# Order of the turnings and of GpSimd's subtraction in a two-stream attention kernel

## The reference

```
xn  = layernorm(x)
# linear attention ("s"), 16 heads of 32
q,k = softmax(ln(xn)@Wq+bq), softmax(ln(xn)@Wk+bk)        # each head by itself
v,p = split(ln(xn)@W_in)
k   = (1-smear)*k + smear*k_of_the_token_before
o   = tril(q k^T * decay) v / (row sum + eps)
s   = ln(silu(p)*o @ W_out)
# local stream ("g"), two layers, 8 heads of 64, windows of 128 tokens and the one before
h   = shift_token(x); q,k,v = split(h@wqkv)
q,k = rotary(l2norm(q)), rotary(l2norm(k))
x   = x + softmax(mask(8 q k^T)) v @ wo
h   = ln(shift_token(x)); x = x + (a*gelu(g))@w2,  a,g = split(h@w1+b1)
out = x_in + s * silu(g stream)
```

## Time and profile before

| | |
|---|---|
| median of 3 runs | 1975.97 us (1974.36 to 1982.03) |
| the profiled execution's own time | 1983.42 us |
| its span | 1981.6 us |
| TensorE matmul busy | 1906.0 us, 96% |
| TensorE weight loads busy | 1645.8 us, 83% |
| VectorE busy | 1732.8 us, 87% |
| ScalarE busy | 1224.2 us, 62% |
| GpSimd busy | 1018.6 us, 51% |
| granted TensorE clock | 0.995 |

### The profile page before, as it was taken

The page is one execution under the profiler, slowest core; times in us unless marked ns, Lnnn a source line. Parts: engine busy times, 40 slices in busy tenths (PEclk is TensorE's granted clock), DMA queues, the critical chain, the costliest instruction groups (busy, mean ns, idle before and its releaser), DMA issues.

```text
span 1981.6 us, 49031 instructions
## 1 busy us (share of the span) xinstructions
PE 1906.0 (96%) x15178; PEld 1645.8 (83%) x15178; DVE 1732.8 (87%) x5212; ACT 1224.2 (62%) x2926; POOL 1018.6 (51%) x1004
## 2 busy tenths in 40 slices
PE   5899999999999999999999999999999999999998
PEld 3788888888888888888788888888888888888887
DVE  5888899898889898889888898889899898898896
ACT  4565656656656656656666567566566566566564
POOL 2545555556556555555444455454554554454552
PEclk8999999999999999999999999999999999999999
DMA  5010000000000100000111111110111111111101
GB/s 199 20 33 21 29 25 22 30 29 22 25 29 21 32 29 21 26 26 25 65 62 47 40 34 41 34 32 29 42 32 40 37 32 29 40 34 34 37 26 33
DMA packets 81152, 72.76 MB, mean 37 GB/s; under 512 B 13484, under 2 KB 74344, under 8 KB 81096
## 3 DMA queue, kind: packets, MB, share of 16 engines
q1 hardware_dynamic: 81096, 72.05, 11.8%
HBM read 42.64 MB, written 16.78 MB: 30 GB/s over the span
## 4 chain that ended last, share of the span: by engine, by line
PE 61%; issue 12%; DVE 12%; ACT 6%; POOL 6%; DVEq 1%; DMA 1%; SPq 0%; POOLq 0%; ACTq 0%
PE bank L1521 36%; PE bank L1526 14%; PE bank L1533 10%; ACT L944 2%; POOL rot_other L707 2%; PE bank L1568 2%; POOL mix_work L715 2%; DVE rot L1413 1%; DVE prob L1048 1%; ACT gel L944 1%; DVE mix_work L1431 1%; POOL small_h L663 1%; DVE sq_sum L1305 1%; POOL small_y L663 1%; DVE mix_work L1112 1%
## 5 line engine op out<-in xcount | busy, mean ns | idle before, releaser
L1521 PE MATMUL bank<-hT_n,w_s 128*128 128x128 f32 x3072 | 402.2, 281 | 1.6 <-ACT hT_n L907 0.9
L1521 PEld LDWEIGHTS bank<-hT_n,w_s 128*128 128x128 f32 x3072 | 364.7, 191 | 35.2 <-issue 21.4
L824 ACT ACTIVATE prob<-prob,row_min 128x256 f32<-128x256 f32 x512 | 256.7, 504 | 171.2 <-DVE row_min L1048 169.6
L1526 PE MATMUL bank<-wqkv_s,xT 128*128 128x512 f32 x1152 | 319.2, 413 | 4.6 <-DVE wqkv_s L1225 1.8
L663 POOL TENSOR_TENSOR inv_norm<-sq_clip,half_neg 128x8 f32<-128x8 f32 x128 | 270.3, 2112 | 55.5 <-DVE sq_clip L1308 55.4
L707 POOL TENSOR_TENSOR rot_other<-raw,rot_t 128x256 f32<-128x256 f32 x256 | 190.2, 774 | 150.0 <-ACT raw L793 150.0
L1526 PEld LDWEIGHTS bank<-wqkv_s,xT 128*128 128x128 f32 x1152 | 207.4, 191 | 53.6 <-DVE wqkv_s L1225 3.8
L1048 DVE CUSTOM_DVE_ANT_0 prob<-bank,table,inv_norm 128x256 f32<-128x256 f32 x512 | 226.5, 479 | 3.9 <-issue 3.6
L1521 PE MATMUL bank<-w_s,hid 128*128 128x256 f32 x768 | 202.3, 387 | 0.0
L793 ACT ACTIVATE pT<-bank 128x512 f32<-128x512 f32 x256 | 139.7, 606 | 30.3 <-PE bank L1533 30.2
L1533 PE MATMUL bank<-table,prob 128*128 128x128 f32 x1024 | 144.9, 274 | 2.3 <-DVE prob L1067 2.3
(11 more groups left out here) (180 smaller groups left out, 4313.6 us busy)
## 6 DMA issues: line engine op xcount, KB each, us to landing
k_prev<-k_carry SPq DMA_DIRECT2D x32, 224.0 KB, 2.5
x_s<-in_L_attn_x SPq DMA_DIRECT2D x32, 128.0 KB, 2.1
rot_s<-in_rotary SPq DMA_DIRECT2D x64, 64.0 KB, 2.0
rows_normalised<-xh SPq DMA_DIRECT2D x32, 128.0 KB, 1.7
y_n<-rows_normalised SPq DMA_DIRECT2D x32, 128.0 KB, 2.1
x_between_layers<-x SPq DMA_DIRECT2D x32, 128.0 KB, 1.7
s_between_passes<-s_out SPq DMA_DIRECT2D x32, 128.0 KB, 1.7
x_s<-x_between_layers SPq DMA_DIRECT2D x32, 128.0 KB, 2.1
```

Source lines behind the costliest of these rows:

```text
L824: ins = act.activation(prob[:, h, :], prob[:, h, :], ACT.Exp, bias=row_min[:, c:c + 1], scale=-1.0, accum_out=row_sum[:, c:c + 1])
L1521: return pe.matmul(out, lhsT, rhs, start=first, stop=last)
L1526: ins = pe.matmul(out, halved(left[:, a]), halved(right[:, b]), start=first and n == 0, stop=last and n == 2)
```

## The change

In `body` of TensorE the groups of turnings come in the order linear queries, local queries, linear keys; the two tiles of the MLP's second product, which stood behind the linear queries, stand behind the output projection. ScalarE copies them out in the same order. VectorE evicts the linear values right behind the square sums, and clips the square sums in the odd iteration only after the key weights. GpSimd subtracts the maxima ahead of its four rotary products. Nothing is computed that was not before, and no operation is added.

```diff
--- before.py
+++ after.py
@@ -328,14 +328,14 @@
         score_bank = [mix_bank[0], mix_bank[1], att_bank[0], att_bank[2]]
 
 
-        mix_pe = Steps(sem("mix_pe"), "q k v kt qt s0 s1 s2 s3 p o0 o1 gt wout")
+        mix_pe = Steps(sem("mix_pe"), "q k v qt kt s0 s1 s2 s3 p o0 o1 gt wout")
         state_pe = Steps(sem("state_pe"), "st0 st1")
         state_dve = Steps(sem("state_dve"), "st0 st1")
         state_pool = Steps(sem("state_pool"), "sdec")
         rows_pe = Steps(sem("rows_pe"), "xt")
         rows_dve = Steps(sem("rows_dve"), "xl")
-        mix_act = Steps(sem("mix_act"), "xt exp kt qt tanh gt")
-        mix_dve = Steps(sem("mix_dve"), "q k max sum kinv kw v kadd "
+        mix_act = Steps(sem("mix_act"), "xt exp qt kt tanh gt")
+        mix_dve = Steps(sem("mix_dve"), "q k max v sum kinv kw kadd "
                         "s2 qsum qeps s3 s0 s1 p den0 rec0 o0 den1 rec1 o1 go "
                         "ystat yaggr yvar")
         y_dve = Steps(sem("y_dve"), "yn")
@@ -695,6 +695,12 @@
                     pool.tensor_tensor(rot_t[:, :, :, :],
                                        rot_s[:, p, :, :].unsqueeze(2).to_broadcast([P, 4, 2, HD // 2]),
                                        rot_scale[layer(u)][:, :, :, :], ALU.mult).then_inc(proj_pool.done("table"), 1)
+                if one is not None:
+                    n = one
+                    pool.wait_ge(mix_dve.sem, mix_dve.at("max", n))
+                    qk_h = qk.rearrange("p (h d) -> p h d", d=MD)
+                    pool.tensor_tensor(qk_h, qk_h, qk_max[:, :].unsqueeze(2).to_broadcast([P, 2 * MH, MD]),
+                                       ALU.subtract).then_inc(mix_pool.done("sub"), 1)
                 if proj is not None:
                     u = proj
 
@@ -708,12 +714,6 @@
                                                      rot_t[:, 2 + a, s, :].unsqueeze(1).to_broadcast([P, H, HD // 2]),
                                                      ALU.mult)
                     ins.then_inc(proj_pool.done("other"), 1)
-                if one is not None:
-                    n = one
-                    pool.wait_ge(mix_dve.sem, mix_dve.at("max", n))
-                    qk_h = qk.rearrange("p (h d) -> p h d", d=MD)
-                    pool.tensor_tensor(qk_h, qk_h, qk_max[:, :].unsqueeze(2).to_broadcast([P, 2 * MH, MD]),
-                                       ALU.subtract).then_inc(mix_pool.done("sub"), 1)
                 if one is not None:
                     n = one
                     pool.wait_ge(mix_dve.sem, mix_dve.at("kw", n))
@@ -964,17 +964,17 @@
                 if m is not None:
                     last_gates(m)
                 if one is not None:
-                    act.wait_ge(mix_pe.sem, mix_pe.at("kt", one))
-                    copy(kT_mix[:, :, :], mix_bank[0][:, :].rearrange("p (g i) -> p g i", g=MG))\
-                        .then_inc(mix_act.done("kt"), 1)
+                    act.wait_ge(mix_pe.sem, mix_pe.at("qt", one))
+                    copy(qT_mix[:, :, :], mix_bank[1][:, :].rearrange("p (g i) -> p g i", g=MG))\
+                        .then_inc(mix_act.done("qt"), 1)
                 if proj is not None:
                     act.wait_ge(proj_pe.sem, proj_pe.at("qt", proj))
                     copy(halved(qT[:, 0, :, :]), proj_bank[:, :].rearrange("p (g i) -> p g i", g=HP))\
                         .then_inc(proj_act.done("qt"), 1)
                 if one is not None:
-                    act.wait_ge(mix_pe.sem, mix_pe.at("qt", one))
-                    copy(qT_mix[:, :, :], mix_bank[1][:, :].rearrange("p (g i) -> p g i", g=MG))\
-                        .then_inc(mix_act.done("qt"), 1)
+                    act.wait_ge(mix_pe.sem, mix_pe.at("kt", one))
+                    copy(kT_mix[:, :, :], mix_bank[0][:, :].rearrange("p (g i) -> p g i", g=MG))\
+                        .then_inc(mix_act.done("kt"), 1)
                 if proj is not None:
                     act.wait_ge(proj_pe.sem, proj_pe.at("kt", proj))
                     copy(halved(kT[:, 0, :, proj.parity, :]), proj_bank[:, :].rearrange("p (g i) -> p g i", g=HP))\
@@ -1304,6 +1304,8 @@
                 dve.wait_ge(proj_act.sem, proj_act.at("square", u))
                 dve.tensor_reduce(sq_sum[:, :], rot[:, :].rearrange("p (h d) -> p h d", d=HD), AX_X, ALU.add)\
                    .then_inc(proj_dve.done("sqsum"), 1)
+            def square_clip(u):
+
                 dve.wait_ge(proj_dve.sem, proj_dve.at("sqsum", u))
                 dve.tensor_scalar(sq_clip[:, :], sq_sum[:, :], 1e-24, None, ALU.max)\
                    .then_inc(proj_dve.done("clip"), 1)
@@ -1377,6 +1379,9 @@
                     scores("b1", a, att_bank[0])
                 if one is not None:
                     square_sums(u)
+                    dve.wait_ge(mix_pe.sem, mix_pe.at("v", one))
+                    dve.tensor_tensor(v_mix[:, :, 0:MD], heads(mix_bank[0][:, :]), heads(bias_mix[:, 0, :]),
+                                      ALU.add).then_inc(mix_dve.done("v"), 1)
                 if f is not None:
                     finish_u(f)
                     if one is None:
@@ -1387,6 +1392,7 @@
                     mix_read(two, 0)
                 if u is not None and one is None:
                     square_sums(u)
+                    square_clip(u)
                 if a is not None:
                     weigh("b1", a)
                 if one is not None:
@@ -1400,11 +1406,9 @@
                     dve.tensor_tensor(k_smear[:, :], k_norm[:, :], smear_s[:, :], ALU.mult)
                     dve.tensor_tensor(k_keep[:, :], k_norm[:, :], keep_s[:, :], ALU.mult)\
                        .then_inc(mix_dve.done("kw"), 1)
+                    square_clip(u)
                     if f is not None:
                         finish_out(f)
-                    dve.wait_ge(mix_pe.sem, mix_pe.at("v", one))
-                    dve.tensor_tensor(v_mix[:, :, 0:MD], heads(mix_bank[0][:, :]), heads(bias_mix[:, 0, :]),
-                                      ALU.add).then_inc(mix_dve.done("v"), 1)
                 if a is not None:
                     low_out(a, 0, "pva", "la")
                 if u is not None:
@@ -1810,21 +1814,21 @@
                 if m is not None and one is None and i.low != UNITS:
                     mlp_out(m, 0, 2)
                 if one is not None:
+                    pe.wait_ge(mix_act.sem, mix_act.at("exp", one))
+                    pe.wait_ge(mix_dve.sem, mix_dve.at("k", one))
+                    transposes(mix_bank[1], [qk[:, g * P:(g + 1) * P] for g in range(MG)])\
+                        .then_inc(mix_pe.done("qt"), 1)
+                if u is not None:
+                    turn_q(u)
+                if one is not None:
                     pe.wait_ge(mix_dve.sem, mix_dve.at("kadd", one))
                     pe.wait_ge(mix_dve.sem, mix_dve.at("v", one))
                     transposes(mix_bank[0], [qk[:, ME + g * P:ME + (g + 1) * P] for g in range(MG)])\
                         .then_inc(mix_pe.done("kt"), 1)
-                if u is not None:
-                    turn_q(u)
-                if one is not None:
-                    pe.wait_ge(mix_act.sem, mix_act.at("exp", one))
-                    pe.wait_ge(mix_dve.sem, mix_dve.at("k", one))
-                    transposes(mix_bank[1], [qk[:, g * P:(g + 1) * P] for g in range(MG)])\
-                        .then_inc(mix_pe.done("qt"), 1)
-                    if m is not None:
-                        mlp_out(m, 0, 2)
                 if a is not None:
                     out_projection(a, att_bank[1])
+                if m is not None and one is not None:
+                    mlp_out(m, 0, 2)
                 if i.low == UNITS:
 
                     hidden(m, mlp_bank[0], 2, 4, 2).then_inc(mlp_pe.done("ga"), 1)
```

## The result

| | before | after |
|---|---|---|
| median of 4 runs each | 1977.12 us (1974.36 to 1982.03) | 1953.74 us (1948.87 to 1955.20) |
| ratio, 95% interval | | 0.9875 (0.9848 to 0.9901) |
| the profiled execution, span | 1983.42, 1981.6 us | 1948.87, 1947.0 us |
| VectorE busy, GpSimd busy | 1732.8, 1018.6 us | 1734.0, 1060.6 us |

The change is faster by 23.4 us (1.2%) by the medians, 20 to 30 us by the interval. The forecast was 30 us (1946). Whole runs differ by more than the terms in question, so the experiments are read by another measure: the length of a steady pair of iterations, from one start of the linear query projection (`wq_s`) on TensorE to the next. In the kernel before it is 59.85 us in the first layer (the twelve pairs lie between 59.82 and 59.90) and 60.11 in the second (60.07 to 60.14). After, it is 59.43 and 58.98.

A forecast was written before the change was run, and what follows sets the result against it. TensorE was taken to bound the kernel, itself bound in the odd iteration by VectorE's way to `kadd`. Gains of 10.4, 15.0 and 5 us, taken as 30, came off the median 1975.97: 1946 us, range 1936 to 1967.

The forecast's parts named there:

- The order, 0.91 a pair: TensorE, odd iteration: two groups of turnings move into the gap before the linear keys, gaining 0.91 us even if `kadd` stays.
- even with VectorE unchanged this wait is met, by 0.0 to 0.1 us: TensorE's local key turnings, asked at 1215.22, find the queries' low part ready, as it ends at 1215.09.
- `kadd` earlier by 0.1 to 0.2: VectorE's addition of the shifted linear keys, for which TensorE waits, ends 0.1 to 0.2 us earlier.
- The term of the weighings: VectorE's two weighings of the last heads, beside the last two rotary products, take 1.4 to 1.6 us.
- The second bound: The DMA of the shifted keys, second landing near 1211.65, lets `kadd` end no earlier than about 1212.3.
- The second layer, 14 by 1.07: Fourteen second-layer pairs of iterations gain 1.07 us each, 15.0 us in all.
- The first layer, 13 by 0.8: Thirteen first-layer pairs gain 0.8 us each, 10.4 us in all; the gap of 0.70 to 0.89 goes whole.
- `xh`, whose race with the subtraction I had bounded: VectorE's first-layer step behind the maxima: 0.4 us or less; if it loses, held 1.9 us and gain 0.5, not 0.8.
- The MLP's move, at nothing: TensorE: the MLP's second matmul group goes behind the output projection, the same work, with VectorE's residual input earlier.
- Edges, 5: Five edge pairs of iterations gain 1.0 us each, 5 us in all.
- The second and fourth: Rivals: the gap only moves, nothing won, 1976 us, chance 0.09; more than forecast, up to 40.4 us, 1936, chance 0.08.
- Of the first: Rival: part of the gain is lost to VectorE, last weighing 0.3 to 0.5 us late; gain 14 us, 1962, chance 0.15.

The follow-up runs named there:

- e5: The changed kernel with GpSimd's decayed keys made to wait for VectorE's scaling of the local keys: pairs 58.90 and 58.72 us, ratio 0.9796.
- e6: The changed kernel with the local queries' two rotary products ahead of GpSimd's subtraction: pairs 58.60 and 59.16 us, one run of 1937.82 us.
- e10: The changed kernel with the MLP's two tiles back ahead of the output projection: pairs 59.53 and 59.64 us, one run of 1966.64 us.

## Why the prediction was right, and where not

The direction and the main mechanism were right, the range (1936 to 1967) held the time, and the size was too large by 7 us by the medians (30 against 23), or by 1 to 6 at an equal clock.

- *The order, 0.91 a pair.* It gave 0.61 and 0.65. In the second layer the step that failed is "even with VectorE unchanged this wait is met, by 0.0 to 0.1 us": the weight loads of the local key turnings wait 0.4 us, and 0.26 of the gain is gone. In the first layer the gap (0.70 to 0.89) set the limit, as forecast, and a wait for L1112 in the even iteration took 0.28 of matmul idle back. For the second layer the lines were there to read: the norm in front of the low part missed `k_dec` by 0.08 us, and the decayed queries behind it waited for the very copy that the change makes earlier. I had priced VectorE's steps up to `kadd` and left those behind it as they were. The prediction named this wait as "what is late next", and a new wait of the local keys above 0.3 us as a sign of being wrong. By the weight loads that sign came in the changed kernel, with about 0.45 in each odd iteration of both layers; as idle time of the matmuls it doesn't show.
- *`kadd` earlier by 0.1 to 0.2.* It came 0.49 earlier. The term of the weighings (1.37 in the second layer, 1.49 in the first, forecast 1.4 to 1.6) was close, that of the clip (0.17) right. Too dear were the cosines: forecast at 1.98, they took 1.35, since they now started first and `k_keep` waited. The addition behind them then took 1.95 in place of 1.23. The second bound, that the DMA lets `kadd` end no earlier than 1212.3, was too late as well: counted from the pair's start, it now ends where 1211.97 was, with no idle time ahead of it.
- *The second layer, 14 by 1.07.* Measured 1.13, so the number came out by luck, from two errors of opposite sign: 0.26 less for the order, about 0.3 more for `kadd`.
- *The first layer, 13 by 0.8.* Measured 0.42 in twelve; this is the mis-sized term, about 5 us. The step said that the gap goes whole. It does, but about 0.4 us come back in the next, even iteration, where TensorE waits for L1048 and L1112. Two rows of VectorE and two of TensorE, first layer, after:

```profile
653.11 0.68 DVE L1435 TENSOR_TENSOR mix_work<-mix_work,k_prev 128x512 f32<-128x512 f32 x1
...
655.08 1.18 DVE L1447 TENSOR_TENSOR rot<-rot,inv_norm 128x512 f32<-128x512 f32 x1
```

```profile
663.54 0.98 PE L1572 MATMUL bank<-kT,qT 64*128 64x256 f32 x12 [0.21 <-DVE row_min L1048]
664.79 1.67 PE L1530 MATMUL bank<-win_s,xhT 128*128 128x512 f32 x6 [0.27 <-DVE mix_work L1112]
```

The norm (1.18) is held by `k_dec`, which here runs from 654.66 to 655.71, since the roots ahead of it end later than before. With that taken away (e5) the pair loses 0.53, with the weighings free as well (e6) 0.83. Either is more than the 0.38 that is missing from 0.8. `xh`, whose race with the subtraction I had bounded, won it:

```profile
642.59 0.35 DVE L1034 TENSOR_SCALAR xh<-xn,small_x 128x256 f32<-128x256 f32 x1
...
646.17 1.49 DVE L1067 TENSOR_SCALAR prob<-prob,row_inv 128x256 f32<-128x256 f32 x2
```

- *The MLP's move, at nothing.* It costs nothing, and it is needed, which the prediction did not see: e10 shows that these tiles, left ahead of the output projection, would have cost 0.66 in the second layer.
- *Edges, 5.* Measured 8.2, part of it the clock.
- *The other signs.* TensorE's matmuls wait for `kadd` no more, but for one place in the first layer. The clip lasts 0.17 in all 54 cases of the two steady stretches. The exponential's wait for GpSimd (6.8 us in 14 in the second layer before) is gone. The pairs got shorter by 0.42 and 1.13, where 0.8 and 1.1 were forecast.
- *The rivals.* The second and fourth did not come. Of the first, the last weighing was not what TensorE waited for, but its idea (part of the gain lost to VectorE) is what happened in the first layer, behind `kadd`.
## What to carry to other kernels

When a gap closes, price the steps behind it as well as those in front: list, for the engine that will be next late, each instruction that starts within a microsecond of one on the engine that shares its port, and ask which of the two starts first. A wait that lets GpSimd start later can be worth as much as a new order: one added wait gave 0.53 and 0.26 us a pair here, in the first layer more than the whole change (0.42). Where whole runs spread by some tenths of a per cent, compare the length of a steady loop pass: within one trace it repeated within 0.1 us here, and its median tells parts of 0.1 us apart.

## What was not expected of the hardware

- Small steps are held too, to the end of GpSimd's operation: a step on 128x16 lasted 0.57 beside a 0.73 us GpSimd addition, and 0.18 when 0.7 us of other work was put ahead of it, so 0.68 us more work cost 0.23 us.
- Steps that read one input from the matmul banks did not stretch beside GpSimd: 0.68 for L1383 at 1182.45 and for L1243 at 1194.41, the first beside a rotary product, the second beside the decayed queries.
- A gain can be taken back by a change that gains alone: in the first layer the subtraction's move is worth 0.32 us without the new order of turnings and costs 0.18 with it.
